# Gate and up as a 2x2 block product with seven block products, in two sweeps of 1024 tokens, on one Trainium2 core

## What is computed

```python
def _L0_cond_ref(u, length, ...):            # H = 64 channels
    mask = (jnp.arange(Lq) < length[:, None])
    kernel = _get_kernel(...)                # [64, 1024], a sum of 64 damped oscillations
    y = causal_convolution(u * mask, kernel) + u * mask * D[:, None]
    return y * mask[:, None, :]
def _L1_cond_ref(x, ...):                    # F = 2752, rank 16, scale 0.5
    gate = lora_add(x @ W_gate.T, x, A_gate, B_gate)
    up = lora_add(x @ W_up.T, x, A_up, B_up)
    act = silu(gate) * up
    return lora_add(act @ W_down.T, act, A_down, B_down)
x = x + _L0_cond_ref(x, ...)
x = x + _L1_cond_ref(x, ...)                 # 2048 tokens (batch, channel) of 1024 features
```

## Time and profile before

| | |
|---|---|
| median of 3 runs | 1822.17 us (1819.97 to 1824.09) |
| the profiled execution: its span | 1824.1 us, 25107 instructions |
| the same execution's own time, the highest of the three runs | 1824.09 us |
| PE (matmul) busy | 1764.9 us, 97% |
| PEld (weight load) busy | 1478.0 us, 81% |
| VectorE, ScalarE, GpSimd busy | 682.0, 506.6, 108.7 us |
| moved by DMA | 285.87 MB, 157 GB/s over the span |

### The profile page before, as it was taken

The page is one execution under the profiler, slowest core; times in us unless marked ns, Lnnn a source line. Parts: engine busy times, 40 slices in busy tenths (PEclk is TensorE's granted clock), DMA queues, the critical chain, the costliest instruction groups (busy, mean ns, idle before and its releaser), DMA issues.

```text
span 1824.1 us, 25107 instructions
## 1 busy us (share of the span) xinstructions
PE 1764.9 (97%) x8728; PEld 1478.0 (81%) x8728; DVE 682.0 (37%) x855; ACT 506.6 (28%) x575; POOL 108.7 (6%) x170
## 2 busy tenths in 40 slices
PE   1999699999999999999999999999999999999999
PEld 1999588888888888888888888888888888888887
DVE  6454343333333433333333433333433433333321
ACT  2220233232322333323322332323222323232221
POOL 6000455300000000000000000000000000000000
PEclk9999899999999999999999999999999999999999
DMA  8988887633365533333455433333555433333442
GB/s 289 346 292 278 276 248 233 191 107 110 98 207 184 162 107 114 101 115 98 133 193 182 146 114 103 113 104 100 162 186 178 135 108 107 110 105 98 124 134 76
DMA packets 162500, 285.87 MB, mean 157 GB/s; under 512 B 29506, under 2 KB 88706, under 8 KB 161666
## 3 DMA queue, kind: packets, MB, share of 16 engines
q1 hardware_dynamic: 112770, 220.05, 38.0%
q10 hardware_dynamic: 36256, 39.59, 6.7%
q0 software_dynamic: 13440, 25.86, 4.4%
HBM read 261.91 MB, written 49.05 MB: 170 GB/s over the span
## 4 chain that ended last, share of the span: by engine, by line
PE 95%; DMA 2%; DVE 1%; ACTq 1%; ACT 0%; issue 0%; SPq 0%; DVEq 0%
PE ps L431 87%; PE ps L409 7%; DMA tt<-k_pad 1%; DMA k_pad<-ksb 1%; ACTq L677 1%; ACTq L252 0%; ACT xhi L534 0%; PE ps L396 0%; DMA leni<-len 0%; DVE sm_ep L728 0%; ACT whi L534 0%; DVE mask L860 0%; DVE xt L901 0%; DVE sm_e2p L728 0%; DVE ksb L822 0%
## 5 line engine op out<-in xcount | busy, mean ns | idle before, releaser
L893 DVE TENSOR_TENSOR wlo<-raw,whi 128x1280 fp32r<-128x1280 f32 (+2 forms) x268 | 369.9, 1381 | 773.7 <-ACT whi L534 773.5
L534 ACT ACTIVATE whi<-raw 128x1280 fp32r<-128x1280 f32 (+3 forms) x288 | 333.5, 1158 | 952.7 <-PE ps L431 878.0
L431 PE MATMUL ps<-xhi,whi 128*128 128x512 f32 (+1 forms) x1440 | 564.7, 392 | 11.2 <-DVE xlo L1014 11.2
L431 PE MATMUL ps<-xhi,wlo 128*128 128x512 f32 (+1 forms) x1440 | 565.1, 392 | 0.0
L431 PE MATMUL ps<-xlo,whi 128*128 128x512 f32 (+1 forms) x1440 | 561.9, 390 | 0.0
L431 PE MATMUL ps<-acts,whi 128*128 128x512 f32 (+1 forms) x1648 | 479.1, 373 | 0.0
L431 PEld LDWEIGHTS ps<-acts,whi 128*128 128x128 f32 x1648 | 298.7, 188 | 62.7
L431 PEld LDWEIGHTS ps<-xhi,whi 128*128 128x128 f32 x1440 | 272.2, 189 | 66.7 <-DVE xlo L1014 12.7
L431 PEld LDWEIGHTS ps<-xhi,wlo 128*128 128x128 f32 x1440 | 271.9, 189 | 64.0
L431 PE MATMUL ps<-acts,wlo 128*128 128x512 f32 (+2 forms) x912 | 318.6, 365 | 0.0
L431 PEld LDWEIGHTS ps<-xlo,whi 128*128 128x128 f32 x1440 | 272.6, 189 | 56.3
(11 more groups left out here) (120 smaller groups left out, 451.5 us busy)
## 6 DMA issues: line engine op xcount, KB each, us to landing
raw<-wgu SPq DMA_DIRECT2D x168, 512.0 KB, 3.7
tt<-k_pad SPq DMA_DIRECT2D x64, 512.0 KB, 5.9
raw<-wd SPq DMA_DIRECT2D x128, 256.0 KB, 2.8
raw<-bgu_sel SPq DMA_DIRECT2D x336, 64.0 KB, 3.4
bgu_sel<-bgu POOLq DMA_DIRECT2D x32, 336.0 KB, 5.6
raw<-wd SPq DMA_DIRECT2D x32, 320.0 KB, 2.9
xres<-x_keep ACTq DMA_DIRECT2D x32, 256.0 KB, 2.8
out<-xres ACTq DMA_DIRECT2D x32, 256.0 KB, 2.1
```

Source lines behind the costliest of these rows:

```text
L431: return nc.tensor.matmul(out, w, x, start=start, stop=stop, skip_group_check=True)
L534: return nc.scalar.activation(out, in_, ACT.Copy)
L893: V.tensor_tensor(wlo[:, slot, 0:w * P], raw[:, slot, 0:w * P], whi[:, slot, 0:w * P].bitcast(F32), ALU.subtract).then_inc(s_wlo, 1)
```

## The change

The reduction dimension of gate and up (8 tiles of 128 features) is cut into two halves of four tiles; with it (gate, up) x (first half, second half) of the weights is a 2x2 block matrix A, and (first half, second half) x (256 tokens g=0, 256 tokens g=1) of x a 2x2 block matrix B. The product of the two takes seven block products instead of eight, in the form of Strassen and Winograd. A block product is 4 tiles x 3 passes of 256 columns. The adapter products stay at 256 columns (8 for each 512 tokens and tile of F).

- Two sweeps of 1024 tokens (A and B of 512 each) for gate and up. All seven x blocks (B11, B21, B12, B22 and the differences T1 to T4), hi and lo, for both 512s stay in SBUF; three of the four weight combinations per tile of F are made on VectorE (`sums_13`, `sums_24`) from the raw gate and up weights, which are now loaded 42 x 2 times instead of 168.
- The results are put together on ScalarE and VectorE: `c1`, `v`, `d`, `c2`, `c12`, then silu and `mul`. P6 waits for `c1`, P4 for `d`, P3 for `v`.
- The activations of each tile go to HBM as f32 (`acts_d`), and the four down sweeps of 512 tokens read them back into a ring of 28 tiles, which ScalarE and VectorE split again.
- Convolution: the reversed input (`xr`) feeds PE, and a second copy of the input in natural order (`xt`) lies ready; 1 is added to tap 0, and `evacuate` is one predicated copy of PSUM over `xt` under the mask, so no sum with x follows. Each quarter of x1 is stored to HBM by SP.
- The adapters of the first two sweeps are gathered at the start, those of down last. All loops are written out.

The diff, cut to what the prediction speaks of (line numbers are not those of the profile of before):

```diff
-            def conv(hq, i, first=False):
...
-                V.tensor_tensor(out, ps[i % NCV][:, 0:C * B].rearrange("p (c g b) -> p c g b", c=C, g=G),
-                                mask[:].rearrange("p c (g b) -> p c g b", g=G), ALU.mult).then_inc(s_cev, 1)
...
+QUAD = {"B11": 0, "B21": 1, "T1": 2, "T3": 3, "T2": 4, "T4": 5, "B22": 6}
+MOVING = {"P1": "B11", "P2": "B21", "P5": "T1", "P7": "T3", "P6": "T2", "P4": "T4", "P3": "B22"}
+STATIONARY = {"P1": (0, 0), "P2": (0, 4), "P5": (1, 0), "P7": (1, 4), "P6": (2, 0), "P4": (2, 4), "P3": (3, 0)}
+RAWS = ("B11", "B21", "B12", "B22")
+RAWS_B = ("B21", "B22", "B11", "B12")
...
...
+        def ring_free(m):
+            if m < NRING:
+                s = m
+                x, q = ("B", s // 2) if s < 14 else ("A", s // 2 - 7)
+                return s_p, prod(N - 1, PRODUCTS[q], x)
+            return s_rel, m - NRING + 1
...
+            reversed_in(0)
+            rows_in(0)
+            reversed_in(1)
...
+            sp.wait_ge(s_kst, 16)
+            for h in range(HG):
+                toeplitz(h, h)
+            for q in range(1, HQ):
+                rows_in(q)
...
+            def toeplitz_group(g):
+                sp.wait_ge(s_kst, 16 * (g + 1))
+                for i in range(HG):
+                    sp.wait_ge(s_conv, HG * (g - 1) + i + 1)
+                    toeplitz(HG * g + i, i)
+            def x1_store(q):
+                sp.wait_ge(s_cev, HH * (q + 1))
+                sp.dma_start(x1_d[:, :, q], xt[:, :, q]).then_inc(s_x1st, 16)
...
+            toeplitz_group(1)
+            for q in range(1, HQ):
+                toeplitz_group(2 * q)
+                if q + 1 < HQ:
+                    reversed_in(q + 1)
+                x1_store(q - 1)
+                if q == HQ - 1:
+                    sp.wait_ge(s_gat, 2 * GU_SEL)
+                    load_ag(0, "A", 0)
+                    load_ag(0, "A", 1)
+                toeplitz_group(2 * q + 1)
+            wait_lo("agA0", 0)
+            load_raw(("wl", 0), wl_d)
+            wait_lo("agA1", 0)
+            load_ag(0, "B", 0)
+            wait_lo("wl", 0)
+            load_ag(0, "B", 1)
+            x1_store(HQ - 1)
+            sp.wait_ge(s_x1st, 16 * HQ)
+            sp.wait_ge(s_xform, xform(0, "A", "T4"))
...
+            def second():
+                sp.wait_ge(s_gat, 4 * GU_SEL)
+                wait_lo("u2", FT - 1)
+                sp.wait_ge(s_s24, 2 * FT)
+                for x in "AB":
...
+            def load_act(j, t):
+                m = KT * j + t
+                sp.wait_ge(*ring_free(m))
+                rows = P if t < FT else FR
+                sp.dma_start(draw[0:rows, m % NRING, :], acts_d[j, t, 0:rows]).then_inc(s_dld[m % NRING], 16)
...
+            def lora_a(u, x):
...
+                    pe.wait_ge(s_c12, 2 * (FT * u - 2) + i + 1)
+                for g in range(2):
+                    pe.wait_ge(s_wlo, UNIT[f"ag{x}{g}", u])
+                    if g == 0:
+                        pe.wait_ge(s_xlo, max(xsplit(u, x, "B11"), xsplit(u, x, "B21")))
+                    else:
+                        pe.wait_ge(s_xlo, max(xsplit(u, x, q) for q in RAWS))
+                    done(block_of(u, x, ps[4 + 2 * i], g, g))
...
+            def products(n):
+                u, f = n // FT, n % FT
...
+                    q = MOVING[p]
+                    a, b = wide_of(n, x)
+                    out = {"P1": half(a, 1), "P6": half(a, 1), "P5": half(a, 0), "P3": half(a, 0),
+                           "P2": half(b, 1), "P7": half(b, 0), "P4": half(b, 0)}[p]
...
+                        pe.wait_ge(s_wlo, UNIT[f"u{slot}", n])
+                    if f == 0:
...
+                    if p == "P6":
+                        pe.wait_ge(s_c1, 2 * n + i + 1)
+                    if p == "P4":
+                        pe.wait_ge(s_d, 2 * n + i + 1)
+                    if p == "P3":
+                        pe.wait_ge(s_v, 2 * n + i + 1)
+                    for k in range(4):
+                        w = (w3hi, w3lo) if slot == 3 else (whi[:, slot], wlo[:, slot])
+                        at = slice((k0 + k) * P, (k0 + k + 1) * P)
+                        last = passes(out, w[0][:, at], w[1][:, at], x_tile(u, x, q, True, k),
+                                      x_tile(u, x, q, False, k), k == 0 and p in ("P1", "P2"))
...
+                    if p == "P7":
+                        if x == "A":
+                            pe.wait_ge(s_wlo, UNIT["lora", n])
+                        if f == 0:
+                            pe.wait_ge(s_tsa, 2 * (2 * u + i + 1))
+                            pe.wait_ge(s_tlo, 3 * (2 * u + i + 1))
+                        last = lora(half(b, 1), 0, 0)
+                    if p == "P4":
+                        lora(half(b, 0), 1, 0)
+                        last = lora(half(b, 1), 1, 1, start=True)
+                    if p == "P3":
+                        last = lora(half(a, 0), 0, 1)
+                    done(last)
+                for p in PRODUCTS:
+                    for x in "AB":
+                        product(p, x)
...
+            for n in range(N):
+                if n % FT == 0:
+                    u = n // FT
+                    lora_a(u, "A")
+                    rest_main(u, "A")
+                    lora_a(u, "B")
+                    rest_lora(u, "A")
+                    rest_main(u, "B")
+                    rest_lora(u, "B")
+                products(n)
...
+                    ins.then_inc(s_dn, 1)
+                def main(c):
+                    if c >= 2 or j:
+                        pe.wait_ge(s_ye, C * j + c - 1)
+                    bank = ps[4 + c % 2]
...
+                            if c == 0:
...
+                            last = passes(bank[:, :], tile(whi, w % 3, k), tile(wlo, w % 3, k), dhi[:, at, :],
+                                          dlo[:, at, :], t == 0)
+                            if c == C - 1:
+                                last.then_inc(s_rel, 1)
...
+                main(0)
+                if j:
+                    pe.wait_ge(s_tde, 3 * (j - 1) + 1)
+                down_a()
+                main(1)
+                tail(0)
+                tail(1)
+                for c in range(2, C):
+                    main(c)
+                    tail(c)
...
+            for n in range(N):
+                if n % FT:
+                    for x in "AB":
+                        silu(n - 1, x)
+                w_hi("u3", n)
+                w_hi("lora", n)
+                if n == N - 1:
+                    gu_to_down()
+                elif n == FT - 1:
+                    again()
+                else:
+                    w_hi("u0", n + 1)
+                    for x in "AB":
+                        c1(n, x)
+                    w_hi("u1", n + 1)
+                    for x in "AB":
+                        v(n, x)
+                    w_hi("u2", n + 1)
...
+            maskbits = mask[:].bitcast(I32).rearrange("p c (g b) -> p c g b", g=G)
+            def evacuate(h):
+                hq, i = h // HH, h % HH
+                dve.wait_ge(s_conv, h + 1)
+                if i == 0:
+                    dve.wait_ge(s_xq[hq], 16)
+                out = xt[:, :, hq, :, i * BG:(i + 1) * BG].rearrange("p g c b -> p c g b")
+                V.copy_predicated(out, maskbits, ps[h % NCV][:, 0:C * B].rearrange("p (c g b) -> p c g b", c=C, g=G)
+                                  ).then_inc(s_cev, 1)
...
+            def sums_13(n):
+                ra, rb = raw_slot(("gate", n)), raw_slot(("up", n))
...
+                V.tensor_tensor(s13[:, 0:512], raw[rb][:, 0:512], raw[rb][:, 512:KB], ALU.add).then_inc(s_s13, 1)
+                sub(s13[:, 512:KB], raw[ra][:, 0:512], raw[rb][:, 0:512]).then_inc(s_s13, 1)
...
+                sub(raw[rb][:, 0:512], s13[:, 0:512], raw[ra][:, 0:512]).then_inc(s_s24, 1)
...
+                sub(s4[:, :], raw[ra][:, 512:KB], raw[rb][:, 0:512]).then_inc(s_s24, 1)
...
+            def d(n, x):
+                i = GRP[x]
...
+                V.tensor_tensor(gq[i][:, 0:512], cc[i][:, :], wide_of(n, x)[1][:, :], ALU.add).then_inc(s_d, 1)
+            def c2(n, x):
...
+                V.tensor_tensor(up[i][:, :].rearrange("p (a n) -> p a n", a=2),
+                                wide_of(n, x)[1][:, :].rearrange("p (a n) -> p a n", a=2),
+                                vv[i][:, :].unsqueeze(1).broadcast_to([P, 2, 256]), ALU.add).then_inc(s_c2, 1)
+                dve.wait_ge(s_c2, 2 * n + i + 1)
+                V.tensor_tensor(up[i][:, 256:512], up[i][:, 256:512], gq[i][:, 0:256], ALU.add).then_inc(s_c2b, 1)
...
+                V.tensor_tensor(gq[i][:, 512:768], wide_of(n, x)[0][:, 0:256], vv[i][:, :], ALU.add).then_inc(s_c12, 1)
...
+                V.tensor_tensor(up[i][:, :], gq[i][:, 256:768], up[i][:, :], ALU.mult).then_inc(s_mul, 1)
...
+            for q in RAWS:
+                x_lo(0, "A", q, "post")
+            w_lo("wl", 0)
+            for q in RAWS_B:
```

(89 more changed lines are left out.)

1551 lines of the change are left out of this document (1046 added, 505 removed).

## The result

The kernel after takes 1774.65 us (median of 4 runs, 1773.73 to 1776.81), the kernel before on the same chip 1822.61 us: a ratio of 0.9741, 95% interval 0.9729 to 0.9753. It is 48 us faster; the forecast was 88 us. The time lies in the range of 1703 to 1785, and the sign and the reason held; 40 us of sizes did not.

The account below looks back on a forecast made before the run. The prediction took PE, matmul price times count, as the bound. Terms -110.0 + 11 - 5.3 + 12 + 4 = -88.3 us took the profiled 1824.1 to 1735.8, 1734 as median; range 1703 to 1785.

Parts of the forecast that it names:

- Gate and up on PE: Gate and up matmuls: seven narrow block products replace the work of eight, other engines keep up; -110.0 us.
- The price of a matmul: All PE matmuls: 0.2333 us at 512 columns and 0.1177 at 256, carried over from the earlier trace.
- Convolution: Convolution: PE work unchanged, predicated copy hidden, ninth Toeplitz load late behind other loads; +11 us, bounds 0 and 21.
- the burst: Convolution: SP issues 6.3 MB of input right behind the first eight Toeplitz loads; the ninth lands near 70 to 72 us.
- Head of the first sweep: From the convolution's end (T) to the first product, near T + 42.5 us: -5.3 us, bounds -16 and +7.
- Between the sweeps: Change between the two gate and up sweeps: PE waits while x comes back and is split; +12 us, bounds 5 and 25.
- Down: Down sweeps: activation tiles arrive in time, the third output tile waits 1.0 us for `y_out` in each sweep; +4 us.
- The step from gate and up to down has its tiles in time: Start of down: activation tiles arrive with 2.9 us or more to spare; cost 0.
- Weight loads one after the other: Rival: narrow matmuls on PE pay for their weight loads, 0.188 us each, +509 us, 2243 us; chance 7%.
- The small waits at many products: Rival: small waits at 588 product boundaries, or activation loads too slow; 1752 to 1764 us, both 1782; chance 22%.
- the counters: Counters PE must look at for each of 588 block products: taken as 0, bound some 0.03 us each, 18 in all.
- the slow copy: Rival: the convolution's predicated copy takes 2 us and VectorE bounds it; +30 us, 1764 us; chance 8%.

Follow-up runs that it names:

- the experiment with later rows: Changed kernel with its three natural-order input loads issued in channel groups 1, 2 and 4 instead of together behind the first Toeplitz loads: 1767.77 us, ratio 0.9704.
- the joint products: Changed kernel with both 512-token halves of each block product issued as one 512-column matmul, one adapter product added to a wrong quarter: 1734.6 us, ratio 0.9524.

## Why the prediction was right or wrong

- **Gate and up on PE**, the mechanism: right. The count of matmuls is the time, VectorE and ScalarE kept up (280.99 and 168.43 us in 461), no boundary between products costs anything.
- **The price of a matmul**, the step that failed most: "Two narrow ones cost 0.2354, 1% more than one wide one. This ratio decides". The prices of the earlier trace rows were right for the kernel before, and I carried them over as if they belonged to the width. They belonged to the places of its buffers. In the kernel after the ratio is 2 x 0.1200 to 0.2267, 6%. That cost 18 us in gate and up and gave back 2 us in each down sweep. Shown by moving buffers alone, in both kernels and in both directions. With weights and x placed nearest to before (hi weights and x as there, lo weights not) the changed kernel takes 1747 us, 13 above the forecast; that is no proof of the 0.1177, since its narrow ones cost 0.1145.
- **Convolution**, +11: the burst was where it was put, and PE wanted the ninth Toeplitz load at 61.8 us, but it landed some 7 us later than the 70 to 72 taken. SP spent 17.52 us in issuing `rows_in`; the ninth load left it at 56.6 as before, behind the burst's bytes. Measured +19.9; the experiment with later rows gives back 8.7 of them, and the cause of the rest is open. The predicated copy took 0.44 us, as its nearest row had it, and bounds nothing.
- **Head of the first sweep**: T + 42.66 against T + 42.5, though by compensation in part: the store of x1 took 12.56 us where I took 11. The two waits in the first tile, 0.74 us and then 2.03 for `c1`, which stands behind the store of the last 64 rows (5.40 us in the chain), were not in the working.
- **Between the sweeps**, +12: measured 17.8. PE is idle for 12.9, where 5 to 6 were expected, and the rest is the lower clock behind the gaps (twice 6.8 us at 0.50). I took x from HBM as there in time; its loads were issued from 710.5 us on, behind the stores of activations, and VectorE stood 9.54 us for them with `d` behind. `d` first gives 1.6 us.
- **Down**: +1.0 a sweep against 0.92. That activation tiles are in time from sweep to sweep held, although 256 KB took 6.9 us in the median to land and not the 2.8 of the earlier trace rows. "The step from gate and up to down has its tiles in time" failed: 0.69, 1.38 and 3.20 us. The last is for adapter weights whose loads stand on SP behind 22 activation loads and behind the store of the last tile's activations. SP has issued the 22 at 1239.9 us and then waits 9 us for VectorE's `mul` of that tile (1248.10 in the chain), which itself stands behind the splits of activation tiles that landed late (7.14 us). The slack was worked out for the tiles and not for what is queued behind them.
- **Rivals.** Weight loads one after the other, 0.188 us a matmul, are refuted: 0.1200 was measured and 0.1133 reached. A floor stands close below, 0.112 at 192 and 128 columns; whether it is the weight load's is not shown. "TensorE: Matmul & The Clock Gate" of the Trainium skill (Back-to-back issue gap) has 131 ns at 512 columns, and an estimate between its figures gave 98 ns at 256; no stream here has narrow ones under 0.113 us or wide ones under 0.22. The small waits at many products (1752 to 1782) named the number that came, but not by its mechanism: the counters cost nothing. That the time lies in the range is in part luck, since its high end stood for that rival and for the slow copy, neither of which happened.

## What to carry to other kernels

When a price per instruction is carried from one kernel to another, ask what else it may depend on; here the same matmul costs 0.2267 or 0.2333, or 0.1133 to 0.1200, by where its operands lie, and moving buffers alone gave 31 and 28 us. Where a change turns wide matmuls into narrow ones, look first whether two narrow ones share their weights: joined they brought 40 us more, on top of the 48. Of a transfer that is "in time" follow also what stands behind it in its queue and behind its consumer.

## What the runs showed of the hardware

- The pace of a saturated stream of weight loads and matmuls depends on the place of the weights relative to that of the moving operand: the same mean at a difference of 0 and 512 bytes (0.1200 narrow, 0.2272 wide), another at 320 (0.1176, 0.2291) and 704 (0.1145, 0.2333), and not on the absolute place, as far as one common shift by 320 bytes shows. Narrow and wide ones want different things: weights at 0 and x at 704 gave the fastest narrow ones (most at 0.1133) and the slower wide ones (0.2333). What VectorE and ScalarE do meanwhile doesn't matter in the kernel after: 0.1200 with one of them busy throughout and with both idle. "TensorE: Matmul & The Clock Gate" of the Trainium skill (Step-by-step: what each phase is for) says that PE has two independent read ports and that loading the next weights takes no bandwidth from the running matmul; these runs don't agree with a reading of that by which placement is free. That the two reads of PE meet in something is likely and not shown; which difference would be best and whether a placement exists that is best for both widths stays open: differences of 0, 320, 512 and 704 were tried, the joint products at 0 alone, and buffers around x and the weights moved with them.
- Below 256 columns a matmul with its own weight load stays at 0.112 us (192 and 128). With 64 columns it was 0.11 at first; then the granted clock went to 0.50 and the starts to 0.21 us, with PE never idle, and it came back when the tiles of 256 columns did.
- At a share of 1.03 the queues moved 408 GB/s from 75 to 100 us in the convolution with later rows, a little above the 388 of the earlier trace rows.
